# A fused decoder layer with expert tiles: one gather, one residual, two weight splits and some routing steps issued in another order

## The reference

```
x = x + linear_attention(layernorm(x))          # 16 heads, elu+1 features, output projection
x = x + cross(layernorm(x), ctx, ctx)           # normalised queries and keys, one kv vector per batch
x = x + moe(layernorm(x))                       # layernorm, gate, top 2 of 8 experts,
                                                # gelu(xn @ W1 + b1) @ W2 + b2, weighted by the gates
```

## Time and profile before

| | |
|---|---|
| median of 3 runs | 436.01 us (435.16 to 436.91) |
| profiled execution, its own time | 435.45 us |
| its span in the trace | 433.5 us |
| PE busy | 406.2 us, 94% of the span |
| DVE, ACT, POOL busy | 341.7, 304.8, 264.6 us |
| mean granted TensorE clock | 0.982 |
| chain that ended last | PE 77%, DVE 6%, POOL 6%, DMA 4%, issue 3%, ACT 2% |

### The profile page before, as it was taken

How to read it: one execution, slowest core, us unless ns; L and a number is a source line. 1 busy time by engine, 2 the same in 40 slices (tenths; PEclk the granted TensorE clock), 3 DMA queues, 4 the chain that set the end, 5 groups by cost and what they waited for, 6 DMA issues and landing times.

```text
span 433.5 us, 8883 instructions
## 1 busy us (share of the span) xinstructions
PE 406.2 (94%) x3001; PEld 381.5 (88%) x3001; DVE 341.7 (79%) x836; ACT 304.8 (70%) x599; POOL 264.6 (61%) x358
## 2 busy tenths in 40 slices
PE   6998999999999999989987999999999999999970
PEld 5887898988989788889987999999999999999970
DVE  5555678778787999788666788979999899979950
ACT  4664667575666776494498788889889798889720
POOL 4356568677776867668865646657656673664331
PEclk9899999999999999999998999999999999999995
DMA  8911020303010612954699697997989889995531
GB/s 272 338 48 30 1 73 26 100 1 99 30 46 26 235 47 50 394 206 153 214 305 342 134 316 192 319 344 221 367 274 309 262 287 284 312 313 143 170 38 12
DMA packets 32337, 79.48 MB, mean 183 GB/s; under 512 B 4674, under 2 KB 23618, under 8 KB 26404
## 3 DMA queue, kind: packets, MB, share of 16 engines
q1 hardware_dynamic: 23328, 67.81, 44.1%
q0 software_dynamic: 7488, 10.39, 13.0%
q10 hardware_dynamic: 1476, 0.72, 0.6%
HBM read 69.27 MB, written 9.63 MB: 182 GB/s over the span
## 4 chain that ended last, share of the span: by engine, by line
PE 77%; DVE 6%; POOL 6%; DMA 4%; issue 3%; ACT 2%; POOLq 0%; DVEq 0%; ACTq 0%
PE bank L434 58%; PE bank L441 5%; PE bank L670 3%; DMA xg<-xn_rows,idxg 2%; PE bank L743 2%; PE bank L722 2%; PE bank L653 2%; POOL y_ L2181 1%; PE bank L887 1%; PE bank L703 1%; PE bank L752 1%; POOL xg L2116 1%; DMA y_<-yb,idxg 1%; DVE st L1377 1%; DMA y_<-yb,idxs 1%
## 5 line engine op out<-in xcount | busy, mean ns | idle before, releaser
L2181 POOL DMA_INDIRECT y_<-yb,idxs x29 | 60.2, 2077 | 64.4 <-DVE yb L1838 44.5
L434 PE MATMUL bank<-w2h,hh 128*128 128x256 f32 x264 | 76.2, 288 | 1.4 <-issue 1.4
L434 PE MATMUL bank<-xh,w1h 128*128 128x256 f32 x256 | 74.8, 292 | 0.2 <-ACT hf L1248 0.2
L434 PE MATMUL bank<-w2l,hh 128*128 128x256 f32 x264 | 74.7, 283 | 0.0
L434 PE MATMUL bank<-w2h,hl 128*128 128x256 f32 x264 | 74.7, 283 | 0.0
L434 PE MATMUL bank<-xh,w1l 128*128 128x256 f32 x256 | 72.3, 283 | 0.0
L434 PE MATMUL bank<-xl,w1h 128*128 128x256 f32 x256 | 72.3, 282 | 0.0
L2116 POOL DMA_INDIRECT xg<-xn_rows,idxg x39 | 55.4, 1420 | 13.3 <-issue 11.0
L1510 DVE TENSOR_TENSOR w1l<-w1r,w1h 128x1024 fp32r<-128x1024 f32 x46 | 55.9, 1219 | 1.0 <-ACT w1h L1026 0.7
L1786 DVE TENSOR_TENSOR w2l<-w2r,w2h 128x1024 fp32r<-128x1024 f32 x40 | 48.8, 1219 | 6.4 <-ACT w2h L1033 6.4
L434 PEld LDWEIGHTS bank<-w2h,hh 128*128 128x128 f32 x264 | 50.7, 192 | 1.6 <-issue 1.6
(11 more groups left out here) (266 smaller groups left out, 1108.2 us busy)
## 6 DMA issues: line engine op xcount, KB each, us to landing
w1r<-ff_ SPq DMA_DIRECT2D x23, 1024.0 KB, 6.8
w2r<-ff_ SPq DMA_DIRECT2D x23, 1024.0 KB, 7.0
b1r<-b_ SPq DMA_DIRECT2D x7, 512.0 KB, 6.8
bs<-ff_ SPq DMA_DIRECT2D x23, 132.0 KB, 5.4
xn_rows<-xn SPq DMA_DIRECT2D x8, 264.0 KB, 2.2
xin<-x_ SPq DMA_DIRECT2D x8, 256.0 KB, 6.7
cT<-ctxT_ SPq DMA_DIRECT2D x8, 256.0 KB, 5.3
cin<-ctx_ SPq DMA_DIRECT2D x8, 256.0 KB, 4.6
```

The lines of the kernel that those rows point to most:

```text
L434: r = e.matmul(o, a_(t), b_(t), start=first and m == 0, stop=m == n - 1)
L2181: e.indirect_dma_start(out=out[:, :], out_offset=bass.IndirectOffsetOnAxis(ap=at, axis=0), in_=yb[t % 2][:, i, :], in_offset=None, compute ...
```

## The change

It moves calls; no instruction is added and none removed.

- POOL: `gather(5)` (two indirect DMAs) stands ahead of `residual_factors(NB-1)` and `scatter(1, 0)`, and no longer behind both.
- ACT: `residual(NB-1)` stands behind `h_high(3, 1)`, no longer ahead of `gelu(3, 1)`; `w2_high(3, 0)` and `w2_high(3, 1)` stand ahead of `gelu(3, 1)`.
- SP: `load_w2(4)` stands ahead of `write_residual(NB-1)`.
- DVE: `route_b(NB-2)` stands directly behind `own_rank(NB-2)`.
- PE: `rank(NB-2)` ahead of `layer2_piece(0)` and `xpose(1)`; `attended(NB-1)` ahead of `context_sums(NB-1)`; `layer1(0, 1)` ahead of `count(NB-3)`; in turn s = NB-1 `xpose_n(NB-3)` behind `crossed(NB-1, 0)`.

```diff
             load_w1(5)
+            load_w2(4)
             write_residual(NB - 1)
-            load_w2(4)
@@ PE, loop over s
-                if s >= 2:
+                if 2 <= s < NB - 1:
                     xpose_n(s - 2)
                 crossed(s, 0)
+                if s == NB - 1:
+                    xpose_n(s - 2)
@@
                 if s == NB - 1:
                     xpose(0)
+                    attended(s)
                 context_sums(s)
@@
-            attended(NB - 1)
             projected(NB - 1)
             rank(NB - 3)
             layer1(0, 0)
+            layer1(0, 1)
             count(NB - 3)
-            layer1(0, 1)
@@
             second_out(NB - 1)
+            rank(NB - 2)
             layer2_piece(0)
             xpose(1)
-            rank(NB - 2)
@@ ACT
             x_high(4)
-            residual(NB - 1)
+            w2_high(3, 0)
+            w2_high(3, 1)
             gelu(3, 1)
-            w2_high(3, 0)
             h_high(3, 0)
-            w2_high(3, 1)
             gelu(3, 2)
             gelu(3, 3)
             h_high(3, 1)
+            residual(NB - 1)
@@ DVE
             own_rank(NB - 2)
+            route_b(NB - 2)
             x_split(1)
             second(NB - 1)
             weigh(0, 0)
-            route_b(NB - 2)
@@ POOL
             scatter(0, 1)
+            gather(5)
             residual_factors(NB - 1)
             scatter(1, 0)
-            gather(5)
             scatter(1, 1)
```

## The result

The kernel after takes 432.95 us (median of 20 runs, 430.53 to 436.94), the kernel before 435.99 beside it. The ratio is 0.9944, with a 95% interval of 0.992 to 0.9968: faster by 2.4 us (1.4 to 3.5 by the interval; the two medians lie 3.0 apart), where 5.5 had been worked out. One of the 20 runs of before took 2261 us and is left out of the ratio. The time lies in the range that was given, but the forecast and the sum behind it stood for twice the gain. The profiled execution took 431.39 us with a span of 429.3 (before 435.45 and 433.5).

The account below looks back on a forecast made before the run. PE, busy 94%, was taken to bound the kernel. 0.45 + 0.33 + 1.70 + 2.49 + 1.64 - 1.1 = 5.5 us off gave 429.95 from the profiled execution, 430.5 from the median; forecast 430.3, range 428.3 to 433.7.

Parts of the forecast that it names:

- Routing, 0.45: PE by 192 us: attended rows and `rank(6)` up give 0.1 us, `route_b(6)` up 0.35 of the 1.19 before `invert(6)`.
- ACT's order, 0.33 and 1.70: Residual down, W2 splits up: PE's waits go, 0.33 us at `layer1(4, 2)` and 1.70 at `layer2(3, 0)`.
- the gather, 2.49: Before `xpose(5)`: `gather(5)` issued earlier lands before PE wants it, so 2.49 us go.
- The new wait, -1.1: Before `layer1(5, 0)`: ACT's packed list makes `x_split(5)` late, PE waits 1.1 us; bounds 0 and 1.6.
- Slow clock, 1.64: At `layer2(3, 1)`: without the two waits the clock stays up, 2.80 us instead of 4.44, saving 1.64.
- The gather of tile 6, put at nothing: `gather(6)`, wanted by PE at about 234.5, lies there by about 234; no cost in the sum.
- Rival C: `gather(5)`, `gather(6)` or W1 of tile 6 comes 2 to 3 us late; about half the gain, 433.0; chance 0.11.
- and from there PE's list is gapless: From `layer1(5, 0)` on PE has no waits, so the 5.5 us gained reach the end.
- rival E: Loads or scatters co-bound tiles 8 to 22, PE runs into them and gives the gain back: 435.5; chance 0.08.
- SP: `write_residual(7)` waits till 221.8 and holds tile 6's W1 load, landing at 230.3, wanted about 232; cost 0.

Follow-up runs that it names:

- the one relaxed from tile 3: Kernel before; from tile 3 on odd tiles' scatters add to a second buffer and wait only for the tile before the last; final sum left out: ratio 0.9935.
- experiment 10: Kernel before with `gather(t+5)` ahead of the scatters of tile t, for t from 3 on: ratio 0.9978 to before.
- far_before: Kernel before with every gather from tile 8 on issued one tile earlier on POOL: 434.56 us, ratio 0.9994.
- The relaxed kernels: Before and after, odd tiles' scatters to a second buffer, sum left out: from tile 1 0.9883 and 0.9828, from tile 3 0.9935 and 0.9841.
- far_after: Kernel after with every gather from tile 8 on issued one tile earlier on POOL: 430.28 us, ratio 0.991 to before.
- far3_after: Kernel after with every gather from tile 8 on one tile earlier on POOL and three yb buffers instead of two: 430.94 us, ratio 0.9906 to before.

## Why the prediction was right or wrong

- *Routing, 0.45: right in kind.* The two waits changed as forecast (`invert(6)` 0.4 where it was 1.2, `gate_logits(7)` 0.9). Where the clock at 10 to 15 us was 1.00, `xpose(4)` starts at 205.1 in the mean of seven executions without these moves and at 204.4 in six with them, but within these two groups it scatters by 0.5 and 1.3 us. In the timed runs nothing of it can be told.
- *ACT's order, 0.33 and 1.70, and the gather, 2.49.* The waits before `layer1(4, 2)` and `layer2(3, 0)` and the one for the gather of tile 5 are gone; the two halves need each other, which the sum had built in.
- *The new wait, -1.1.* It is 1.01 to 1.03 us in all three traces of after, on DVE's xl, as worked out.
- *Slow clock, 1.64: right in kind, mis-sized.* Of the six executions with before's order at this place and its early waits, three had the slow clock (before, the one relaxed from tile 3, experiment 10) and three had not (the second of before, the routing moves, `far_before`). It is worth 1.5 us at `xpose(6)` where it comes (232.34 to 240.06 is 7.72, 231.57 to 237.78 is 6.21), about 0.8 in the mean. At the end of the span less is left: from `xpose(4)` on, before took 227.5 us with it and 226.9 without. The profiled execution had it, and it also had started 1 us late: its clock was 0.67 at 10 to 15 us. The prediction set one execution's own rows as the rule.
- *The gather of tile 6, put at nothing.* It made PE wait in three of the nine executions with after's order (0.90, 1.45 and 2.49 us), about 0.5 us in the mean. Rival C had named it, at 0.11.
- *The step that failed: "and from there PE's list is gapless", and with it rival E put at 0.08 because there was "not one wait of PE there".* The list of before was gapless only since PE was slow enough. A tile's first scatter waits for the landing of the tile before, and landings took 5.1 to 8.6 us, median 6.7, for the scatters of 280 to 345 us in before. The chain's own pace shows best behind a tile H, which has a single scatter. With the chain relaxed the first scatter of tile 13 starts 6.1 us behind that of tile 12 (H), as the other engines deliver. In after these are 332.94 and 341.91, 9.0 us, with 5.38 us of waiting in between:

```profile
332.94 2.31 POOL L2183 DMA_INDIRECT y_<-yb,idxs  x1 [4.17 <-DVE yb L1840]
341.91 2.03 POOL L2183 DMA_INDIRECT y_<-yb,idxs  x1 [5.38 <-DMA y_<-yb,idxs]
```

  PE, which came earlier, met this chain twice: through gathers queued behind late scatters (1.2 us between the means of before's two executions and after's three) and at the end (1.4 us, from 0 to 4). The relaxed kernels show that both are the chain's; `far_after` shows that the first goes by the gathers. Half of rival E's mechanism was the right one, with scatters in the place of loads.
- *SP.* The later W1 load cost nothing, as forecast.

So of the 3.1 us that are missing (5.5 against 2.4) roughly half was lost ahead of `xpose(6)`, by the slow clock and the gather of tile 6, and roughly half behind it, by the chain. The timed runs don't show this split by themselves: the pairs with the relaxed chain are 0.994 and 0.9905 of each other, within their intervals no more than the change as it is.

Open: why in after the tail is 13.3 in one execution and 17.4 in another at nearly the same lead, and why the slow clock comes in some executions and not in others. No run here controls either.

## What to carry to other kernels

A bottleneck engine without waits shows that the others keep up with its present lateness, not that they would keep up if it came earlier. Before a gain of some us is carried to the end, take each serial chain beside that engine (here scatter, landing, next scatter) and compare its own pace with the engine's; what it has in slack is all that can pass. And two moves in different engines' lists may each be worth nothing or less alone: test the pair. Size terms from more than one execution where the clock or the landing of a transfer is one of them.

## What the runs showed of the hardware

- The same two waits of PE within 7 us (1.43 or 1.44 us, then 1.7 to 2.5) were followed by the lower level (1 us windows at 0.50) in three executions of six, and by 1.00 in three. It also came behind two waits of 0.71 and 1.88 us (the gather alone, 0.50) and during one of 5.69 us (the ACT part alone, 0.50). A single wait of 1.01 to 1.03 us was followed by 1.00 in every trace of after and its variants, also where a second wait of 2.49 us came 5.6 us behind the first (`far3_after`).
- The clock of the start differs between executions of one kernel: 0.67 or 1.00 at 10 to 15 us, and what follows comes about 1 us later or earlier (`xpose(4)` at 206.01 or 204.97 in before, 0.66 and 205.82 in `far_before`).
- Once the weight loads are over, the last scatter still needs 10.3 to 10.6 us from its issue to the end of the span (418.67 to 429.3, 422.56 to 432.9).
